# A fused two-layer block on one core: score blocks of one key tile and two heads, and an add cut in four

## The chip, the cores and the metric

The program runs on one core of a Trainium2 chip. The metric is the device time in microseconds (us) from start to end of one execution; several executions are timed and their median counts. One further execution is recorded by the hardware profiler, and the rows below come from it. The engines are called PE (TensorE, the matrix engine), DVE (VectorE), ACT (ScalarE), POOL (GpSimd) and SP (SyncE, which only issues transfers). Each works through its own queue in order, and they wait for one another by semaphores.

## The reference, cut to what matters

The input is 8 sequences ("batches") of 512 tokens with 256 features. Four blocks are added to it one after the other: an attention with hyperbolic distances, a mixture of 64 experts, a low-rank attention, and an attention with switched value experts. The change touches only the first:

```python
q, k, v = (layernorm(x) @ w.T for w in (wq, wk, wv))      # 16 heads of 16
q_norm_sq, k_norm_sq = sum(q*q), sum(k*k)
diff_sq = q_norm_sq + k_norm_sq - 2.0 * qk
denom = max((1 - q_norm_sq) * (1 - k_norm_sq), 1e-6)
cosh_arg = max(1.0 + 2.0 * diff_sq / denom, 1.0)
attn = softmax(-arccosh(cosh_arg))
x = x + (attn @ v) @ wo.T
```

With t = cosh_arg - 1, the number exp(-arccosh(1 + t)) is 1 / (1 + t + sqrt(t (t + 2))). The kernel computes it as exp(-ln(1 + (t + sqrt(t (t + 2))))).

## The kernel before

The program has three stages. Stage one holds the first attention, the router, the shared expert and the table of expert slots, for all 8 batches; stage two runs the 64 experts; stage three the two other attentions. Only stage one is changed.

Stage one is a software pipeline over batches b = -1 to 9 and, within each, over the 8 pairs of heads (p = 0 to 7). Every engine runs the same loop, `cycle(v, b, par, p, ...)`, and the order of the work on each queue is written out by hand: what a cycle always does, and between it the tasks that the tables `TO_ACT` (products that ACT takes from PSUM) and `TO_DVE` (those that DVE takes) name for that pair. A table's last column says to which batch the task belongs ("this", "before", "after", "before2"): layer norm and projections of the next batch run beside the distances of this one and the router of the one before.

The query and key vectors of a pair lie transposed in `QT` and `KT`: 54 partition rows for the even head from row 0, and 54 for the odd head from row 64 (`SL` = 64). Each head's vector is written as three parts of `QV` = 18 rows, so that a product in the faster format keeps its precision. A matmul of a 128-key tile `KT[lo:hi, pair, mt*P:(mt+1)*P]` with all 512 queries `QT[lo:hi, pair, :]` gives t itself, 128 keys by 512 queries, in one PSUM bank.

The steps of one pair:

- **PE, `scores(v, pair, r)`**, L352: four blocks r = 0 to 3 of two matmuls each, into the two PSUM tiles `SC[0]` and `SC[1]` of two banks. Block r holds head r // 2 and key tiles 0 and 1, or 2 and 3. Before it PE waits on `scores_free`, which says that the block before last was read. Blocks 0 and 1 of the next pair are issued at the end of a cycle, blocks 2 and 3 early in the pair's own.
- **DVE, `distances`**: for each block L614 writes max(t, 0) to `TT`, and L616 (t + 2) t to `SS`. `TT` is a ring of 8 heads, `SS` one of 4. `room` waits once for a pair until the ring places are free: on `pv` (attention product done) and on `w` (POOL's add done for the pair before last). `distances_slow` is the branch for clamped denominators and isn't taken with these inputs.
- **ACT, `root(v, h)`**, L780, one cycle later: square root of `SS` for one head, 128 x 2048, after `scores_free` has counted that head's two blocks.
- **POOL, `add_root(v, h)`**, L849: `TT` = `TT` + `SS` for one head, one instruction of 128 x 2048; it then increments `w`. Around it POOL has the scatter of slot numbers (L853, indirect DMAs) and two small powers for the layer norms (L843).
- **ACT, `logarithm`** (L784) and **`numerator`** (L788), another cycle later, in `TT`.
- **PE, `attend`**, L373: four steps a pair, one key tile of both heads each, summed in `OB`. `query_norms` (L359) makes one matmul for either head, at rows 0 to 53 and at rows 64 to 117.

Other work of stage one that the text names: the transposes of queries and keys (`refill`, L340) from `ST`, which DVE's `split` fills (L568 a cast, L570 and L571 differences, four instructions for a pair); transposes (L301) into `WKA`, which ACT copies to `XT` (L792); the shared expert's products (`shared`, L433 and L434, taken by DVE at L751); the projection of queries and keys (`project`, L307); `norms` (L509 to L520); `clamp_apply` (L537 to L555); `stats` and `norm` (L478 to L488, with POOL's L843 between them); and the slot numbers (`slots`, L700 to L730).

Of the kernel before, what the change touches and what calls it, by code (L numbers as in the profile page):

```python
# [19 lines left out]
ALU = mybir.AluOpType  # L20
# [3 lines left out]
P = 128  # L24
B, N, D = 8, 512, 256
T = B * N
NT = N // P
# [4 lines left out]
GH = 4  # L32
NG = H0 // GH
QV = DH0 + 2
SL = 64
RING = 2 * GH
CLAMP = 1e-6
# [33 lines left out]
class View:  # L71
# [77 lines left out]
    p=H0, pv=H0, o_sb=NG, ao=1, x1=1, var2=1, rstd2=1, xn2=1, mask=1, shifted=1, exps=1,  # L149
# [5 lines left out]
def stage_one(nc, sems, sb, ps, dram, cst, TIDF):  # L155
# [10 lines left out]
    SQ = sb("SQ", [P, 2, N])  # L166
    ST = sb("ST", [P, 2, 2, 2 * NT, SL])
    QT = sb("QT", [P, PAIRS, N], F32R)
    KT = sb("KT", [P, PAIRS, N], F32R)
    V = [sb(f"VAL{i}", [P, NT, H0, DH0 + 1]) for i in range(2)]  # L170
    TT = sb("TT", [P, RING, NT, N])
    SS = sb("SS", [P, GH, NT, N])
# [18 lines left out]
    AM = [sb(f"AM{i}", [P, 2, PAIRS, NT, 2]) for i in range(2)]  # L191
# [12 lines left out]
    SC = [ps(f"SC{i}", [P, 2, N]) for i in range(2)]  # L204
# [18 lines left out]
    def a_slot(v, parts, par, p, slot, **of):  # L223
        for at, s, name, i, whose in TO_ACT:
            if at == p and s == slot and of[whose]:
                parts[name](v, i, par)
# [6 lines left out]
    def bank_d(v):  # L233

        v.items += 1
        return WKD[v.items % 2]

    block = nc.Block()
    with block as block:
# [43 lines left out]
        def _(pe):  # L283
# [57 lines left out]
                                       ST[:, pair % 2, side, 2 * j:2 * j + 2, :].rearrange("p a b -> p (a b)"), ident[:])  # L341
                ins.then_inc(sems["refill_in"], 1)

            def scores(v, pair, r):

                h2, half = r // 2, r % 2
                lo, hi = SL * h2, SL * h2 + 3 * QV
                if v.due("scores_free", 2):
                    pe.wait_ge(sems["scores_free"], v.value)
                for m in range(2):  # L350
                    mt = 2 * half + m
                    ins = pe.matmul(SC[half][:, m, :], KT[lo:hi, pair, mt * P:(mt + 1) * P], QT[lo:hi, pair, :],  # L352
                                    start=True, stop=True)
                ins.then_inc(sems["scores"], 1)

# [116 lines left out]
        def _(dve):  # L472
# [97 lines left out]
                dve.tensor_tensor(q_st[:, :, 2 * QV:3 * QV], q, q_st[:, :, 0:QV], ALU.subtract)  # L570
                dve.tensor_tensor(k_st[:, :, QV:2 * QV], k, k_st[:, :, 0:QV], ALU.subtract).then_inc(sems["split"], 1)  # L571

            def room(v, h2):

                if h2 == 0 and v.due("pv", RING, 2):
                    dve.wait_ge(sems["pv"], v.value)
                if h2 == 0 and v.due("w", GH, 2):
                    dve.wait_ge(sems["w"], v.value)

            def distances_slow(v, par, pair):  # L580

                dve.wait_ge(sems["work_d"], v.next("work_d", 2))
                for h2 in range(2):
                    dve.tensor_scalar(SQ[:, h2, :], bank_d(v)[:], -1.0, 1.0, ALU.mult, ALU.add).then_inc(sems["took_d"], 1)
                dve.drain()
                for h2 in range(2):
                    h = 2 * pair + h2
                    tt, ss = TT[:, h % RING], SS[:, h % GH]
                    room(v, h2)
                    for half in range(2):  # L590
                        dve.wait_ge(sems["scores"], v.next("scores"))
                        for m in range(2):
                            mt = 2 * half + m
                            dve.tensor_scalar(ss[:, mt, :], SQ[:, h2, :], AM[par][:, 1, pair, mt, h2:h2 + 1], CLAMP,
                                              ALU.mult, ALU.max)
                            dve.drain()
                            dve.reciprocal(ss[:, mt, :], ss[:, mt, :])
                            dve.drain()
                            dve.scalar_tensor_tensor(tt[:, mt, :], SC[half][:, m, :], 0.0, ss[:, mt, :], ALU.max, ALU.mult)
                            dve.drain()  # L600
                            ins = dve.scalar_tensor_tensor(ss[:, mt, :], tt[:, mt, :], 2.0, tt[:, mt, :], ALU.add, ALU.mult)
                            dve.drain()
                        ins.then_inc(sems["scores_free"], 1)

            def distances(v, par, pair):

                for h2 in range(2):
                    h = 2 * pair + h2
                    tt, ss = TT[:, h % RING], SS[:, h % GH]
                    room(v, h2)  # L610
                    for half in range(2):
                        part = slice(2 * half, 2 * half + 2)
                        dve.wait_ge(sems["scores"], v.next("scores"))
                        dve.tensor_scalar(tt[:, part, :], SC[half][:], 0.0, None, ALU.max)  # L614
                        dve.drain()
                        dve.scalar_tensor_tensor(ss[:, part, :], SC[half][:], 2.0, tt[:, part, :], ALU.add, ALU.mult)\  # L616
                            .then_inc(sems["scores_free"], 1)
                    if h2 == 0:
                        dve.wait_ge(sems["work_d"], v.next("work_d", 2))
                        dve.sem_inc(sems["took_d"], 2)  # L620

# [154 lines left out]
        @block.scalar  # L776
        def _(act):
            def root(v, h):
                act.wait_ge(sems["scores_free"], v.next("scores_free", 2))
                act.activation(SS[:, h % GH], SS[:, h % GH], ACT.Sqrt).then_inc(sems["root"], 1)  # L780

            def logarithm(v, h):
                act.wait_ge(sems["w"], v.next("w"))
                act.activation(TT[:, h % RING], TT[:, h % RING], ACT.Ln, bias=1.0)  # L784

            def numerator(v, h):
                act.drain()
                act.activation(TT[:, h % RING], TT[:, h % RING], ACT.Exp, scale=-1.0).then_inc(sems["p"], 1)  # L788

            def to_xt(v, c, par):  # L790
                act.wait_ge(sems["work_a"], v.next("work_a"))
                act.activation(XT[:, c, :], WKA[:], ACT.Copy).then_inc(sems["took_a"], 1)  # L792

            def project(v, j, par):
                act.wait_ge(sems["work_a"], v.next("work_a"))
                act.activation(QK[:, :, :, j, :, 0:DH0].rearrange("p s q h d -> p (s q) h d"),
                               WKA[:].rearrange("p (g h d) -> p g h d", h=2, d=DH0), ACT.Copy).then_inc(sems["took_a"], 1)

            def refill(v, i, par):
                act.wait_ge(sems["refill_in"], v.next("refill_in"))  # L800
                act.activation((QT, KT)[i % 2][:, i // 2, :], WKA[:], ACT.Copy).then_inc(sems["took_a"], 1)  # L801

            parts = dict(turn=to_xt, turn_ao=to_xt, turn2=to_xt, turn_hid=to_xt, project=project, refill=refill)

            def cycle(v, b, par, p, **of):
                roots = of["this"] if p else of["before"]
                numerators = of["this"] if p > 1 else of["before"]
                h_root, h_num = 2 * ((p - 1) % PAIRS), 2 * ((p - 2) % PAIRS)
                a_slot(v, parts, par, p, 0, **of)
                if roots:  # L810
                    root(v, h_root)
                a_slot(v, parts, par, p, 1, **of)
                if roots:
                    root(v, h_root + 1)
                a_slot(v, parts, par, p, 2, **of)
                if p == 7 and of["before"]:
                    act.wait_ge(sems["gu"], v.next("gu"))
                    act.activation(GU[:, :, 0:F], GU[:, :, 0:F], ACT.Silu).then_inc(sems["silu"], 1)
                if numerators:
                    act.preload_act_table_set("natural_log_exp_and_others")  # L820
                    logarithm(v, h_num)
                a_slot(v, parts, par, p, 3, **of)
                if numerators:
                    numerator(v, h_num)
                a_slot(v, parts, par, p, 4, **of)
                if numerators:
                    logarithm(v, h_num + 1)
                a_slot(v, parts, par, p, 5, **of)
                if numerators:
                    numerator(v, h_num + 1)  # L830
                if p == 6 and of["before"]:
                    act.wait_ge(sems["shifted"], v.next("shifted"))
                    act.activation(LS[:], LS[:], ACT.Exp).then_inc(sems["exps"], 1)
                a_slot(v, parts, par, p, 6, **of)

            pipeline(cycle)
# [3 lines left out]
        def _(pool):  # L840
# [3 lines left out]

            def add_root(v, h):
                pool.wait_ge(sems["root"], v.next("root"))
                tt = TT[:, h % RING].rearrange("p a b -> p (a b)")
                ss = SS[:, h % GH].rearrange("p a b -> p (a b)")
                pool.tensor_tensor(tt, tt, ss, ALU.add).then_inc(sems["w"], 1)  # L849

            def scatter(v, c0):
                for c in range(c0, c0 + SCATTERS):
# [1008 lines left out]
```

## Time and profile before

| | |
|---|---|
| median of 3 runs | 3386.88 us (3384.12 to 3393.02) |
| the profiled execution's own time | 3382.55 us |
| its span, first to last instruction | 3380.4 us |
| mean granted TensorE clock | 0.814 of full speed |
| PE busy | 2684.0 us, 79% |
| PE weight loads | 1231.3 us, 36% |
| DVE busy | 2039.4 us, 60% |
| ACT busy | 1709.0 us, 51% |
| POOL busy | 1845.2 us, 55% |

Busy shares are means over the span. Stage one ends at about 1500 us. A row of a view by line and form has the line, the engine, the operation, its output and inputs with their shapes, and the count; then busy us and the mean ns of one; then the engine's idle time just before these instructions and what ended it. A row of a timeline has start, duration, engine, line, operation and count, and in brackets the idle time before it with its releaser; neighbours of one kind are drawn together.

### The profile page before, as it was taken

Reading aid. Unit: us, or ns where it says so; the run is one execution under the profiler, and the core shown is the slowest. Engines: PE = TensorE matmul, PEld = TensorE weight load, DVE = VectorE, ACT = ScalarE, POOL = GpSimd, SP = SyncE. Lnnn points to the kernel's source line nnn. Section 1 sums busy time; section 2 is a strip of 40 time slices with the busy share of each in tenths; the row PEclk is TensorE's granted clock in tenths of the full one; section 3 lists DMA queues with packets and bytes.
Section 4 is the critical chain, followed back from the end, with each engine's and each line's share of the span. In section 5 each row is a group of like instructions: output and inputs, shape, how many; then the busy total and the mean of one; then the engine's idle time right before and its main releaser. Section 6 shows DMA issues by size and latency. Waiting matters only on the chain. (4 is left out here: it accounts for less than half of the span.)

```text
span 3380.4 us, 31098 instructions
## 1 busy us (share of the span) xinstructions
PE 2684.0 (79%) x10185; PEld 1231.3 (36%) x10185; DVE 2039.4 (60%) x3044; ACT 1709.0 (51%) x2409; POOL 1845.2 (55%) x1527
## 2 busy tenths in 40 slices
PE   4677787777777677774598499989999999999984
PEld 2222333232332333222255144444444444444432
DVE  4787868687887868662133166564646565655541
ACT  1677667666666767791122154444444444444440
POOL 0444456565655555674577103583847465655585
PEclk7667676676767777666699699999999999999996
DMA  2000000000000000002599400000000000000000
GB/s 88 13 0 1 15 13 13 15 13 15 8 8 13 15 13 7 15 9 27 150 277 240 93 1 1 1 1 19 1 19 1 19 1 13 7 7 1 7 1 13
DMA packets 94880, 99.02 MB, mean 29 GB/s; under 512 B 19552, under 2 KB 91488, under 8 KB 94688
## 3 DMA queue, kind: packets, MB, share of 16 engines
q1 hardware_dynamic: 69984, 73.53, 7.5%
q0 software_dynamic: 24704, 23.22, 3.8%
q8 instruction: 84, 1.38, 0.2%
q14 instruction: 108, 0.88, 0.2%
HBM read 74.24 MB, written 26.80 MB: 30 GB/s over the span
## 5 line engine op out<-in xcount | busy, mean ns | idle before, releaser
L849 POOL TENSOR_TENSOR TT<-TT,SS 128x2048 f32<-128x2048 f32 x128 | 579.6, 4543 | 530.9 <-ACT SS L780 529.8
L1467 ACT ACTIVATE PR<-S,NM 128x512 f32<-128x512 f32 x512 | 347.6, 684 | 591.3 <-DVE NM L1588 591.3
L1588 DVE TENSOR_REDUCE NM<-S 128x2 f32<-128x1024 f32 x256 | 313.1, 1223 | 254.9 <-PE S L1382 254.7
L373 PE MATMUL OB<-TT,VAL 128*17 128x512 f32 x1024 | 386.9, 865 | 75.9 <-ACT TT L788 75.5
L614 DVE TENSOR_SCALAR TT<-SC 128x1024 f32<-128x1024 f32 x256 | 311.8, 1218 | 134.6 <-PE SC L352 75.8
L853 POOL DMA_INDIRECT slot_tokens<-TID,IDX x256 | 261.3, 1021 | 131.0 <-issue 86.8
L1382 PE MATMUL S<-KT,QT 64*128 64x512 f32 x1024 | 328.7, 662 | 0.0
L616 DVE SCALAR_TENSOR_TENSOR SS<-SC,TT 128x1024 f32<-128x1024 f32 x256 | 313.6, 1225 | 20.2 <-issue 1.3
L352 PE MATMUL SC<-QT,KT 54*128 54x512 f32 x512 | 232.6, 554 | 78.2 <-DVE SS L616 77.7
L1411 PE MATMUL OT<-PT,VN 128*64 128x512 f32 x1024 | 283.1, 632 | 3.0 <-ACT PT L1473 2.1
L1393 PEld LDWEIGHTS TP<-ident,PR 128*128 128x128 f32 x2048 | 227.3, 141 | 143.7 <-issue 118.2
L1393 PE MATMUL TP<-ident,PR 128*128 128x128 f32 x2048 | 275.4, 277 | 4.3 <-DVE PT L1593 2.6
L788 ACT ACTIVATE TT<-TT 128x2048 f32<-128x2048 f32 x128 | 244.8, 1912 | 9.2
L784 ACT ACTIVATE TT<-TT 128x2048 f32<-128x2048 f32 x128 | 243.9, 1905 | 0.7
L780 ACT ACTIVATE SS<-SS 128x2048 f32<-128x2048 f32 x128 | 242.0, 1906 | 3.7 <-DVE SS L616 2.9
L1593 DVE COPY PT<-TP 128x512 f32<-128x512 f32 x256 | 175.4, 685 | 102.3 <-PE TP L1393 99.8
L352 PEld LDWEIGHTS SC<-QT,KT 54*128 54x128 f32 x512 | 102.7, 242 | 307.7 <-DVE SS L616 211.1
L1686 POOL TENSOR_TENSOR GT<-AH,MO 128x320 f32<-128x320 f32 x224 | 156.5, 730 | 94.5 <-DVE AH L1618 86.7
L1671 POOL TENSOR_TENSOR VN<-VN,VM 128x256 f32<-128x256 f32 x256 | 186.0, 727 | 37.3 <-issue 1.3
L1651 POOL TENSOR_TENSOR rstd1b<-var1b,mhalf 128x4 f32<-128x4 f32 x16 | 16.5, 1032 | 340.9 <-DVE var1b L1533 340.9
L1473 ACT ACTIVATE PT<-TP 128x512 f32<-128x512 f32 x256 | 153.1, 598 | 57.0 <-PE TP L1393 56.2
L340 PE MATMUL WKA<-ident,ST 128*128 128x128 f32 x512 | 115.5, 366 | 83.4 <-ACT QT L801 53.0
(227 smaller groups left out, 4485.8 us busy)
## 6 DMA issues: line engine op xcount, KB each, us to landing
WG<-w_gu SPq DMA_DIRECT2D x64, 384.0 KB
WD<-w_dn SPq DMA_DIRECT2D x64, 128.0 KB
stream<-rows SPq DMA_DIRECT2D x1, 4224.0 KB, 17.2
XL<-x SPq DMA_DIRECT2D x8, 512.0 KB, 4.2
X<-x SPq DMA_DIRECT2D x8, 512.0 KB, 3.9
rows<-XL SPq DMA_DIRECT2D x8, 512.0 KB
slot_tokens<-TID,IDX POOLq DMA_INDIRECT x256
stream<-X SPq DMA_DIRECT2D x8, 512.0 KB
```

Of the source, the lines that this page charges most:

```text
L352: ins = pe.matmul(SC[half][:, m, :], KT[lo:hi, pair, mt * P:(mt + 1) * P], QT[lo:hi, pair, :], start=True, stop=True)
L373: ins = pe.matmul(OB[r:r + DH0 + 1, :], values_of[:, mt, h, :], TT[:, h % RING, mt, :], start=(mt == 0), stop=(mt == NT - 1))
L614: dve.tensor_scalar(tt[:, part, :], SC[half][:], 0.0, None, ALU.max)
L616: dve.scalar_tensor_tensor(ss[:, part, :], SC[half][:], 2.0, tt[:, part, :], ALU.add, ALU.mult)\
L788: act.activation(TT[:, h % RING], TT[:, h % RING], ACT.Exp, scale=-1.0).then_inc(sems["p"], 1)
L849: pool.tensor_tensor(tt, tt, ss, ALU.add).then_inc(sems["w"], 1)
L853: pool.indirect_dma_start(table, bass.IndirectOffsetOnAxis(ap=IDX[:, c:c + 1], axis=0), TID[:, c // K:c // K + 1], None).then_inc(sems["sc ...
L1382: ins = pe.matmul(S[s % 2][:, h2, :], QT[r % 2][lo:lo + DH1, pair, j * P:(j + 1) * P], KT[r % 2][lo:lo + DH1, pair, :], start=True, stop=True)
L1393: ins = pe.transpose(TP[h2][:, m * P:(m + 1) * P], PR[s % 2][h2][:, m * P:(m + 1) * P], ident[:])
L1411: ins = pe.matmul(OT[lo:lo + DH1, :], VN[r % 2][:, m, h * DH1:(h + 1) * DH1], PT[pair % 2][h2][:, m, :], start=(m == 0), stop=(m == NT - 1))
L1467: act.activation(PR[s % 2][h2][:], S[s % 2][:, h2, :], ACT.Exp, bias=NM[:, s % 2, h2:h2 + 1], accum_out=SM[:, pair % 2, j, h2:h2 + 1]).the ...
L1588: dve.tensor_reduce(NM[:, s % 2, :], S[s % 2][:], AX, ALU.max, negate=True).then_inc(sems["peak"], 1)
```

## The change

A score block holds one key tile of both heads instead of two key tiles of one head. Its two matmuls therefore use different row halves (0 to 53, 64 to 117). DVE's two instructions for a block still have 128 x 1024 elements, now written to two places 2048 elements apart. ACT's `root` waits once for a pair, for all four blocks, before its even head. POOL's add for one head is issued as four instructions of 128 x 512, of which the last increments `w`. The counts of all semaphores stay as they were.

```diff
-            def scores(v, pair, r):
-
-                h2, half = r // 2, r % 2
-                lo, hi = SL * h2, SL * h2 + 3 * QV
+            def scores(v, pair, mt):
+
                 if v.due("scores_free", 2):
                     pe.wait_ge(sems["scores_free"], v.value)
-                for m in range(2):
-                    mt = 2 * half + m
-                    ins = pe.matmul(SC[half][:, m, :], KT[lo:hi, pair, mt * P:(mt + 1) * P], QT[lo:hi, pair, :],
+                for h2 in range(2):
+                    lo, hi = SL * h2, SL * h2 + 3 * QV
+                    ins = pe.matmul(SC[mt % 2][:, h2, :], KT[lo:hi, pair, mt * P:(mt + 1) * P], QT[lo:hi, pair, :],
                                     start=True, stop=True)
                 ins.then_inc(sems["scores"], 1)
...
+            def tiles(pair):
+                h = 2 * pair
+                return TT[:, h % RING:h % RING + 2], SS[:, h % GH:h % GH + 2]
...
             def distances(v, par, pair):
 
-                for h2 in range(2):
-                    h = 2 * pair + h2
-                    tt, ss = TT[:, h % RING], SS[:, h % GH]
-                    room(v, h2)
-                    for half in range(2):
-                        part = slice(2 * half, 2 * half + 2)
-                        dve.wait_ge(sems["scores"], v.next("scores"))
-                        dve.tensor_scalar(tt[:, part, :], SC[half][:], 0.0, None, ALU.max)
-                        dve.drain()
-                        dve.scalar_tensor_tensor(ss[:, part, :], SC[half][:], 2.0, tt[:, part, :], ALU.add, ALU.mult)\
-                            .then_inc(sems["scores_free"], 1)
-                    if h2 == 0:
+                tt, ss = tiles(pair)
+                room(v)
+                for mt in range(NT):
+                    dve.wait_ge(sems["scores"], v.next("scores"))
+                    dve.tensor_scalar(tt[:, :, mt, :], SC[mt % 2][:], 0.0, None, ALU.max)
+                    dve.drain()
+                    dve.scalar_tensor_tensor(ss[:, :, mt, :], SC[mt % 2][:], 2.0, tt[:, :, mt, :], ALU.add, ALU.mult)\
+                        .then_inc(sems["scores_free"], 1)
+                    if mt == 1:
                         dve.wait_ge(sems["work_d"], v.next("work_d", 2))
                         dve.sem_inc(sems["took_d"], 2)
...
             def root(v, h):
-                act.wait_ge(sems["scores_free"], v.next("scores_free", 2))
+                if h % 2 == 0:
+                    act.wait_ge(sems["scores_free"], v.next("scores_free", NT))
                 act.activation(SS[:, h % GH], SS[:, h % GH], ACT.Sqrt).then_inc(sems["root"], 1)
...
             def add_root(v, h):
                 pool.wait_ge(sems["root"], v.next("root"))
-                tt = TT[:, h % RING].rearrange("p a b -> p (a b)")
-                ss = SS[:, h % GH].rearrange("p a b -> p (a b)")
-                pool.tensor_tensor(tt, tt, ss, ALU.add).then_inc(sems["w"], 1)
+                tt, ss = TT[:, h % RING], SS[:, h % GH]
+                for mt in range(NT):
+                    ins = pool.tensor_tensor(tt[:, mt, :], tt[:, mt, :], ss[:, mt, :], ALU.add)
+                ins.then_inc(sems["w"], 1)
```

## Rows read from the trace of the kernel before

**Rows 1.** The page: granted TensorE clock in 40 slices of the span.

```profile
PEclk7667676676767777666699699999999999999996
```

**Rows 2.** Windows: busy us and count of PE, PEld, DVE, ACT, POOL; clock; DMA.

```profile
800.00:990.00 190.00, 146.72 (x441) 60.81 (x441) 147.80 (x220) 129.51 (x96) 108.69 (x51) 0.69 0.07 13
...
1000.00:1022.00 22.00, 21.82 (x50) 7.79 (x50) 9.33 (x9) 8.30 (x9) 6.31 (x3) 0.50 0.07 24
1022.00:1044.00 22.00, 18.32 (x56) 7.05 (x55) 11.18 (x14) 18.58 (x14) 11.64 (x7) 0.97 0.09 25
...
1500.00:3380.00 1880.00, 1579.37 (x6903) 779.22 (x6899) 912.42 (x1388) 709.32 (x1673) 1056.28 (x1172) 0.91 0.16 40
```

**Rows 3.** Waits from 100 to 1500 us: total, times, longest.

```profile
PEld SC L352 <- DVE SS L616: 200.0, 106, 9.5
...
DVE TT L614 <- PE SC L352: 75.8, 39, 8.8
```

**Rows 4.** Lines L359, then L352: durations (min/median/max) and first and last start.

```profile
L359 PE MATMUL WKD<-QT,selq x2: 790/791/792, 999.8 to 999.8; 54*128 54x512 f32 x2
...
L352 PE MATMUL SC<-QT,KT x2: 625/708/792, 1003.6 to 1004.2; 54*128 54x512 f32 x2
```

**Rows 5.** Timeline of PE, 1027 to 1036 us.

```profile
1027.41 1.96 PE L307 MATMUL WKA<-wqkv,XT 128*128 128x512 f32 x4 [1.92 <-ACT QK L796]
...
1035.35 0.73 PE L352 MATMUL SC<-QT,KT 54*128 54x512 f32 x2
```

**Rows 6.** Groups, 100 to 1500 us (L1690: whole span); last row durations as in rows 4.

```profile
L849 POOL TENSOR_TENSOR TT<-TT,SS 128x2048 f32<-128x2048 f32 x126 | 570.6, 4543 | 530.8 <-ACT SS L780 529.8 <-issue 0.6
...
L614 DVE TENSOR_SCALAR TT<-SC 128x1024 f32<-128x1024 f32 x249 | 303.3, 1218 | 134.3 <-PE SC L352 75.8 <-POOL TT L849 50.0 <-issue 8.1
...
L568 DVE CAST ST<-QK 128x288 fp32r<-128x288 f32 x112 | 92.9, 871 | 14.1 <-PE WKA L340 13.9
...
L509 DVE TENSOR_TENSOR SQ<-QK 128x1024 f32<-128x1024 f32 x14 | 31.5, 2248 | 0.5
...
L707 DVE TENSOR_TENSOR LG<-LG,eoff 128x256 f32<-128x256 f32 x7 | 28.0, 3993 | 0.5
...
L548 DVE TENSOR_SCALAR RR<-RR 128x64 f32<-128x64 f32 x7 | 24.9, 3563 | 0.5
...
L514 DVE TENSOR_SCALAR AM<-NR 128x128 f32<-128x128 f32 x7 | 10.2, 1454 | 0.5
...
L1690 POOL TENSOR_TENSOR GO<-GO,GT 128x1280 f32<-128x1280 f32 x56 | 162.1, 2894 | 8.3 <-issue 0.4
...
L568 DVE CAST ST<-QK x128: 292/305/4673, 54.5 to 1354.2; 128x288 fp32r<-128x288 f32 x128
```

**Rows 7.** Timeline of DVE, instructions that stretch and waits at L614.

```profile
182.76 0.97 DVE L568 CAST ST<-QK 128x288 fp32r<-128x288 f32 x1
...
182.76 5.52 DVE L568 CAST ST<-QK 128x288 fp32r<-128x288 f32 x2
...
612.32 3.06 DVE L483 TENSOR_SCALAR var<-mv 128x4 f32<-128x4 f32 x1
...
1036.12 1.23 DVE L614 TENSOR_SCALAR TT<-SC 128x1024 f32<-128x1024 f32 x1 [5.93 <-PE SC L352]
...
1089.58 4.83 DVE L568 CAST ST<-QK 128x288 fp32r<-128x288 f32 x2
...
1149.03 1.23 DVE L614 TENSOR_SCALAR TT<-SC 128x1024 f32<-128x1024 f32 x1 [0.91 <-PE SC L352]
...
1157.04 4.59 DVE L707 TENSOR_TENSOR LG<-LG,eoff 128x256 f32<-128x256 f32 x1
```

**Rows 8.** Timeline of POOL, the adds beside these.

```profile
178.99 9.13 POOL L849 TENSOR_TENSOR TT<-TT,SS 128x2048 f32<-128x2048 f32 x2 [22.86 <-ACT SS L780]
...
610.80 4.55 POOL L849 TENSOR_TENSOR TT<-TT,SS 128x2048 f32<-128x2048 f32 x1 [3.91 <-ACT SS L780]
...
1084.99 9.03 POOL L849 TENSOR_TENSOR TT<-TT,SS 128x2048 f32<-128x2048 f32 x2
```

More of the change, by code:

```diff
@@ L571, in split, with room @@
                 dve.tensor_tensor(k_st[:, :, QV:2 * QV], k, k_st[:, :, 0:QV], ALU.subtract).then_inc(sems["split"], 1)
-            def room(v, h2):
-                if h2 == 0 and v.due("pv", RING, 2):
+            def tiles(pair):
+                h = 2 * pair
+                return TT[:, h % RING:h % RING + 2], SS[:, h % GH:h % GH + 2]
+            def room(v):
+                if v.due("pv", RING, 2):
                     dve.wait_ge(sems["pv"], v.value)
-                if h2 == 0 and v.due("w", GH, 2):
+                if v.due("w", GH, 2):
                     dve.wait_ge(sems["w"], v.value)
@@ L585, in distances_slow @@
                 dve.drain()
-                for h2 in range(2):
-                    h = 2 * pair + h2
-                    tt, ss = TT[:, h % RING], SS[:, h % GH]
-                    room(v, h2)
-                    for half in range(2):
-                        dve.wait_ge(sems["scores"], v.next("scores"))
[L592 to L595, printed above, removed]
-                            dve.drain()
[L597 to L603, printed above, removed]
@@ L605, in distances @@
-            def distances(v, par, pair):
[L607 to L611, printed above, removed]
-                        part = slice(2 * half, 2 * half + 2)
-                        dve.wait_ge(sems["scores"], v.next("scores"))
-                        dve.tensor_scalar(tt[:, part, :], SC[half][:], 0.0, None, ALU.max)
-                        dve.drain()
-                        dve.scalar_tensor_tensor(ss[:, part, :], SC[half][:], 2.0, tt[:, part, :], ALU.add, ALU.mult)\
-                            .then_inc(sems["scores_free"], 1)
-                    if h2 == 0:
+                tt, ss = tiles(pair)
@@ new lines, in distances_slow @@
+                room(v)
+                for mt in range(NT):
+                    dve.wait_ge(sems["scores"], v.next("scores"))
+                    for h2 in range(2):
+                        dve.tensor_scalar(ss[:, h2, mt, :], SQ[:, h2, :], AM[par][:, 1, pair, mt, h2:h2 + 1], CLAMP,
+                                          ALU.mult, ALU.max)
+                        dve.drain()
+                        dve.reciprocal(ss[:, h2, mt, :], ss[:, h2, mt, :])
+                        dve.drain()
+                        dve.scalar_tensor_tensor(tt[:, h2, mt, :], SC[mt % 2][:, h2, :], 0.0, ss[:, h2, mt, :],
+                                                 ALU.max, ALU.mult)
+                        dve.drain()
+                        ins = dve.scalar_tensor_tensor(ss[:, h2, mt, :], tt[:, h2, mt, :], 2.0, tt[:, h2, mt, :],
+                                                       ALU.add, ALU.mult)
+                        dve.drain()
+                    ins.then_inc(sems["scores_free"], 1)
@@ new lines, in distances @@
+            def distances(v, par, pair):
+                tt, ss = tiles(pair)
+                room(v)
+                for mt in range(NT):
+                    dve.wait_ge(sems["scores"], v.next("scores"))
+                    dve.tensor_scalar(tt[:, :, mt, :], SC[mt % 2][:], 0.0, None, ALU.max)
+                    dve.drain()
+                    dve.scalar_tensor_tensor(ss[:, :, mt, :], SC[mt % 2][:], 2.0, tt[:, :, mt, :], ALU.add, ALU.mult)\
+                        .then_inc(sems["scores_free"], 1)
+                    if mt == 1:
@@ L846, in add_root @@
                 pool.wait_ge(sems["root"], v.next("root"))
-                tt = TT[:, h % RING].rearrange("p a b -> p (a b)")
-                ss = SS[:, h % GH].rearrange("p a b -> p (a b)")
-                pool.tensor_tensor(tt, tt, ss, ALU.add).then_inc(sems["w"], 1)
+                tt, ss = TT[:, h % RING], SS[:, h % GH]
+                for mt in range(NT):
+                    ins = pool.tensor_tensor(tt[:, mt, :], tt[:, mt, :], ss[:, mt, :], ALU.add)
+                ins.then_inc(sems["w"], 1)
             def scatter(v, c0):
```

## The prediction

> **What bounds the kernel now.** I read the page first, for where stage one ends and what clock it has: the granted clock is 0.6 to 0.7 in the first 18 slices and mostly 0.9 after [rows 1]. The change touches nothing behind 1500 us, which is 1880 us of the span [rows 2]; all that follows is about the 1500 us before. Then windows of one batch: in 190 us PE is busy 146.7, DVE 147.8, ACT 129.5 and POOL 108.7 [rows 2]. No engine is full. The reader should see two engines at 77% that hand work to each other in queues of fixed order. Then the waits: PE's weight loads for the scores wait 200.0 us for DVE to free a block, and DVE only 75.8 us for scores [rows 3]; POOL waits 529.8 us for ACT's root [rows 6]. So DVE leads PE at most scores, and a faster score block matters where the row of DVE's wait says that PE is late. The timelines show two such places in a batch, and long stretches in which DVE goes from task to task without a wait: those are paid in DVE time.
>
> The third thing to see is in DVE's own durations. A cast of 128x288 takes 305 ns in its median, but 871 ns in the mean of 112; L707 needs 3993 ns for 256 elements a row, L548 3563 ns for 64 [rows 6]. These long ones all lie beside an add of POOL. Undisturbed, L568 has its median; L509, with as many elements as L614, has 1.22 us; L707, L548 and L514, with fewer elements than the cast, have at most its 0.3. Against these the excess of the groups is 59 (92.9 less 112 x 0.305), 14, 26, 23 and 8 us: 130 us, some 16 a batch [rows 6]. L614 and L616, which read PSUM, never stretch: 1218 ns in the mean [rows 6].
>
> **The score blocks.** The trace has both arrangements. In a score block at the lower clock (0.50 of full, the 1.2 GHz level [rows 2]) the matmuls start at 1003.6 and 1004.2, one after the other, and the second lasts 0.63 us [rows 4]: the block takes 1.22 us. The two matmuls of `query_norms`, same shape but in different row halves, start together and end after 0.79 us [rows 4]. So a block falls from 1.22 to 0.79 us at the lower clock; at the full one from 0.73 [rows 5] to about 0.50, half of what the lower level gives up (0.43), since it streams twice as fast. A mean clock of 0.69 [rows 2] is 62% of the time at 0.5; four blocks in 64 pairs are then some 90 us less PE work. Hardly any is on the path:
> - Around 1000 to 1022 us PE is busy 21.82 of 22 us [rows 2]; two blocks of pair 1 lie in that run, and it ends in transposes that ACT waits for; behind ACT's copies come the projection and then DVE's wait, 5.93 us at 1036.12 [rows 7]. Both blocks count: -0.86. The block that ends that wait, at full clock: -0.23.
> - DVE's 0.91 us wait before pair 7 [rows 7] ends with a block at full clock: -0.25.
> - In all other pairs PE waits for DVE to free the block, which costs the gain; worth 0. Were every block on the path it would be 32 x 0.35 = 11 us a batch.
>
> **DVE's two instructions** keep their 1024 elements: 0; the inner runs stay 512 long. ACT's root waits for four blocks instead of two, but comes a cycle later, behind DVE's tasks: 0. If that cover were gone, it would be one block pair, 4.9 us, for each pair; nothing shows it near.
>
> **The add in four.** L849 takes 4543 ns for 2048 elements, L1690 2894 ns for 1280 [rows 6]: 2.15 ns an element and 0.15 us besides. A piece of 512 is then 1.25 us, four are 4.98: +0.44 us a head. Lower bound +0 (4.54 / 4), upper +0.6. POOL idles 530 us before its adds [rows 6], so this is mostly hidden; behind the adds wait L843, the scatters, and DVE's `room`.
>
> What do the cuts do to the stretched DVE instructions? Here the order of turns decides. At 178.99 two adds follow each other; the boundary is near 183.5. DVE's cast comes at 182.76 and needs 0.97 us: it gets in at the boundary. The second cast, ready at once, is then held for the whole second add: both take 5.52 us [rows 7, 8]. So DVE's and POOL's instructions take turns, and each DVE instruction of this kind waits for one POOL instruction as long as POOL has one queued. With pieces, a lone DVE instruction waits 0.6 us in the mean instead of some 3. But a chain of them loses a piece at each member, and POOL's pieces wait in turn. For a chain with as many members as pieces are left, nothing is won, and DVE ends later by what POOL's adds have grown. Place by place, per batch:
> - L483 (612.32, 3.06 us) stands alone [rows 7]; behind it POOL's power for the norm, after the add of 610.80 [rows 8]. That add starts 0.86 us earlier, since two score blocks lie before ACT's root; it grows 0.44 and is held up 0.2. DVE then is bound by the power's result, not by L483: -1.7.
> - L509: two of them with a free instruction between; mean excess 1.0 us over 14 [rows 6], 1.8 a batch. One lands near the end of an add, the second in new pieces: -1.0.
> - L548, then L550, L553 and L555 as further members, four pieces left: 0.
> - L568 at 1089.58, held 4.3 us by the second add of 1084.99 [rows 7, 8]: 4.3 pieces left, eight members (two splits). Blocked time 4.3 + 0.9 of growth, and four members in it; before, these came after it. +1.0. The same at pair 6: +1.0. At pair 5 PE is later anyhow: 0.
> - L707 at 1157.04 and its neighbours, six members and more: +1.0 for the growth [rows 7].
>
> Sum for a batch: -0.86 - 0.23 - 0.25 - 1.7 - 1.0 + 2.0 + 1.0 = -1.1 us, in 8 batches -8.5. Besides, L514 was hit twice in the run for 4.3 us each (10.2 us in seven, against 0.23 each) [rows 6] and stands nearly alone: -5. Together about -13 us. The profiled execution took 3382.55 us for its span of 3380.4; the median shown is 3386.88. Against its own time the forecast is 3370, against the median 3374 us.
>
> Two rules of the Trainium skill bear on this. "SBUF — State Buffer", section "SBUF: two separate sides", says that DVE and GpSimd share a port pair as an exclusive lock held for the whole instruction; read simply, an add a quarter as long blocks a quarter as long, which is what the first rival below would be. "TensorE: Matmul & The Clock Gate", Part 1, says that the slow clock is the resting state and activity lifts it; this speaks against making PE's work denser and its pauses longer, the second rival. The trace agrees only in part: the window at 0.50 has PE busy for 99% of it, the one at 0.97 for 83% [rows 2]. By the first rule alone the time would be 3300 us, by the second alone 3417, against my 3374.
>
> **Rivals.**
> A, *the cuts free DVE*: after its turn DVE keeps the port for its next instructions, or POOL's gap between pieces lets several through. Then each of some 50 hits loses 0.6 us instead of the measured: 130 - 30 = 100 us less DVE time, of which I put three quarters on the path (DVE is busy 78% of a batch [rows 2]), and with PE's terms 3386.9 - 75 - 11 = about 3300. For it: the size of the excess. Against it: the second cast at 182.76. Chance 0.10.
> B, *the clock* (the other side): with less PE work the full-clock stretch of the projections, 1022 to 1044 at 0.97 [rows 2], stays at the lower level. Four products of 1.96 us there become 3.7 each, +7.0 us, of which PE's wait for ACT hides 1.9 [rows 5]: +5.1 us a batch, +41 in all, and with PE's terms 3386.9 + 41 - 11 = 3417. It decides as soon as a batch loses more than 1.5 us of this kind. For it: the low clock in this stage. Against it: what lifts the clock isn't the busy share. Chance 0.13.
> C, *nothing*: PE waits for DVE anyway, gains and growths cancel: 3386.9 less or more 8. Chance 0.30; the same terms as mine, with the add's growth at its upper bound or L483 and L509 gaining half.
> D, *the pieces cost more*: the pool's pieces and DVE's chains meet more often (adds are 10% longer), and the wait at `room` for pair 7, now without any, appears: +1.0 more at each of three chains and 1 us at `room`, +4 - 1 a batch: +24, 3411. Chance 0.07.
> My forecast (a gain of 10 to 35 us, its upper part if more of the 90 us of PE work proves to be on the path) has 0.40.
>
> **How the numbers follow.** A measurement of this kernel tells about 0.3%, 10 us, from no change. A and 0.36 of the forecast's 0.40 are faster: 0.46. C less a little and the forecast's edge are the same: 0.33. B, D and that little are slower: 0.21. The range goes from 3332 (half the PE work on the path, or half of A) to 3407 (half of B): outside it are A's full size and B's, about 2 in 10.
>
> **What would show it.** Score blocks of 0.79 and 0.50 us on PE, L352 starts in pairs; if not, the first step is wrong. L849 x512 at 1.25 us mean. L568's longest near 1.5 us instead of 4.7, but L570, L571, L709 to L715, which never stretched, now at over 1 us in part: that is the turn-taking; if they stay undisturbed, A is right. The clock in windows of a batch near 0.69; under 0.65 is B. DVE busy in stage one nearly unchanged. The prediction fails if PE's chain through ACT was longer on the path than two blocks a batch, or the clock moves.

## The result, and the profile after

The changed kernel takes 3293.97 us in the median of 4 runs (3291.70 to 3321.41), the kernel before 3385.61: a ratio of 0.974, 95% interval 0.969 to 0.980, or some 87 to 92 us less. Forecast were 3374 us and a range of 3332 to 3407. Direction right, size not: seven times as much as the 13 us of the sum.

The page of the changed kernel: the granted clock in 40 slices (against [rows 1]), and POOL's add.

```profile
PEclk7678787877777777775997899999999999999996
...
L848 POOL TENSOR_TENSOR TT<-TT,SS 128x512 f32<-128x512 f32 x512 | 652.1, 1308 | 401.8 <-ACT SS L779 401.5
```

Windows of the changed kernel, columns as in [rows 2]: one 190 us stretch, and the 6 us in which PE has the shared expert's products of one batch.

```profile
670.00:860.00 190.00, 132.79 (x463) 53.95 (x461) 154.12 (x240) 134.59 (x101) 124.80 (x106) 0.74 0.08 15
...
947.00:953.00 6.00, 6.00 (x24) 2.91 (x24) 4.97 (x6) 2.37 (x3) 3.74 (x4) 1.00 0.00 0
```

In a stretch as long as the one of [rows 2], PE is busy 14 us less and DVE 6 us more: more work of DVE fits in. The clock is 0.74, where it was 0.69. The second row has no like in the kernel before. The same products, L433 there and L431 here, by line (min/median/max):

```profile
L433 PE MATMUL WKD<-wdn,XT x48: 634/714/794, 440.8 to 1393.7; 128*128 128x256 f32 x48
```
```profile
L431 PE MATMUL WKD<-wdn,XT x48: 379/431/483, 416.9 to 1311.9; 128*128 128x256 f32 x48
```

All 48 between 100 and 1430 us (eight in each of six batches; L434 there and L432 here have the eight over the other rows) were at the lower clock before, and all 48 are at the full one now: the run of 16 products takes 5.1 us instead of 9.3 in each of these batches. PE's timeline just ahead of it, in the changed kernel:

```profile
942.53 1.90 PE L371 MATMUL OB<-TT,VAL 128*17 128x512 f32 x4 [0.19 <-ACT TT L787]
944.36 0.96 PE L340 MATMUL WKA<-ident,ST 128*128 128x128 f32 x4
...
945.68 1.04 PE L371 MATMUL OB<-TT,VAL 128*17 128x512 f32 x4
...
947.07 0.70 PE L431 MATMUL WKD<-wdn,XT 128*128 128x256 f32 x2
```

The attention step `L371` falls from 1.90 to 1.04 us within 3 us: the clock rises during L340, some 6 us into pair 1. Before, PE had the same work here at 0.50 for all 22 us to 1022 [rows 2].

The pairs of batches 1 to 6, mean us from the first L614 (L612) of a pair to that of the next, read off DVE's timeline of the kernels told of below; with the length of the run of shared products, the projections that follow it ("proj": `project` into WKA, four runs of four matmuls a batch, their lengths summed over the six batches; all at full clock would be 47), DVE's held time (all DVE instructions to 1500 us, what each lasts beyond the shortest of its kind in any of these kernels, where over 0.15 us), and the median. The medians come from several chips: gains are compared with the kernel before on the same chip, and not one median with another.

```
                    p0    p1    p2    p3    p4    p5    p6    p7  batch shared  proj  held  median
before             18.7  25.4  32.5  22.4  16.2  26.4  19.3  27.1  187.9   9.3    53   160    3386
change             16.9  20.7  29.5  21.6  16.5  25.8  19.9  25.5  176.4   5.1    53   140    3294
e1 blocks only     17.5  20.1  33.8  22.8  15.5  25.9  20.2  26.6  182.3   5.1    65   186    3354
e2 pieces only     17.7  26.5  30.9  22.2  17.3  26.8  19.5  26.4  187.4   9.3    57   143    3387
e5 pairs 0, 1      16.9  20.9  30.3  22.2  17.2  26.8  19.3  26.2  179.9   5.1    58   134    3339
e6 pairs 2 to 7    17.6  21.2  29.0  21.6  16.6  25.7  20.1  25.0  176.8   5.1    55   145    3317
e7 before, 1/4 add 16.9  18.8  32.1  20.1  15.2  25.5  19.3  25.3  173.3   5.1    57    15    3292
e9 filler          18.7  21.9  32.8  22.4  16.2  26.5  19.3  27.1  184.8   5.1    59   157    3378
e10 blocks twice   17.4  20.8  29.7  22.1  17.0  25.7  19.5  26.2  178.4   5.1    60   149    3325
```

Of 11.5 us a batch, 4.7 are in pair 1, where the shared products lie, 3.0 in pair 2, 3.4 in pairs 0 and 7.

The clock moves at a second place too. In the six batches of the changed kernel the projections behind the shared products are at full clock four times; twice their second and third run are mostly at the lower one:

```profile
961.51 3.19 PE L307 MATMUL WKA<-wqkv,XT 128*128 128x512 f32 x4 [3.65 <-ACT QK L795]
965.47 3.66 PE L307 MATMUL WKA<-wqkv,XT 128*128 128x512 f32 x4 [0.78 <-ACT QK L795]
```

A run of four takes 1.95 us at full clock ([rows 5] has one). In these two batches DVE's wait for scores in pair 2 is 7.7 us, in three others 4.7: what the projections take longer is on the path. The kernel before has them all at full clock in three of its six batches.

### The profile page after: what moved, and what is told of

The parts are those of the page before. It is cut to its first block and busy times, and to the rows that moved or that the text cites. A ratio compares the mean times of both kernels' runs of the same rounds, so it can differ in the third digit from the quotient of the medians.

```text
span 3289.6 us, 31482 instructions
## 1 busy us (share of the span) xinstructions
PE 2514.8 (76%) x10185; PEld 1158.7 (35%) x10185; DVE 2017.9 (61%) x3044; ACT 1706.0 (52%) x2409; POOL 1914.4 (58%) x1911
## 5 line engine op out<-in xcount | busy, mean ns | idle before, releaser
L848 POOL TENSOR_TENSOR TT<-TT,SS 128x512 f32<-128x512 f32 x512 | 652.1, 1308 | 401.8 <-ACT SS L779 401.5
L371 PE MATMUL OB<-TT,VAL 128*17 128x512 f32 x1024 | 349.4, 786 | 86.9 <-ACT TT L787 86.9
L612 DVE TENSOR_SCALAR TT<-SC 128x1024 f32<-128x1024 f32 x256 | 311.4, 1216 | 121.4 <-POOL TT L848 60.7
L614 DVE SCALAR_TENSOR_TENSOR SS<-SC,TT 128x1024 f32<-128x1024 f32 x256 | 313.5, 1225 | 20.2 <-issue 1.3
L350 PE MATMUL SC<-QT,KT 54*128 54x512 f32 x512 | 149.6, 594 | 96.1 <-DVE SS L614 95.9
L340 PE MATMUL WKA<-ident,ST 128*128 128x128 f32 x512 | 115.0, 365 | 114.9 <-ACT QT L800 78.2
L1690 POOL TENSOR_TENSOR GO<-GO,GT 128x1280 f32<-128x1280 f32 x56 | 161.9, 2892 | 8.2 <-issue 0.4
```

The source lines that it names most:

```text
L371: ins = pe.matmul(OB[r:r + DH0 + 1, :], values_of[:, mt, h, :], TT[:, h % RING, mt, :], start=(mt == 0), stop=(mt == NT - 1))
L612: dve.tensor_scalar(tt[:, :, mt, :], SC[mt % 2][:], 0.0, None, ALU.max)
L614: dve.scalar_tensor_tensor(ss[:, :, mt, :], SC[mt % 2][:], 2.0, tt[:, :, mt, :], ALU.add, ALU.mult)\
L848: ins = pool.tensor_tensor(tt[:, mt, :], tt[:, mt, :], ss[:, mt, :], ALU.add)
```

## The experiments

Each was timed beside the kernel before on its chip, whose median there was 3390 (e1 to e4), 3391 (e5 to e8), 3392 (e9 to e12) and 3397 us (e13 to e15); ratios are to that.

**The two halves apart.** e1 is the changed kernel with POOL's add whole, e2 the kernel before with the add in four.

```diff
 # e1                                        # e2: the other way round
-                for mt in range(NT):
-                    ins = pool.tensor_tensor(tt[:, mt, :], tt[:, mt, :], ss[:, mt, :], ALU.add)
+                pool.tensor_tensor(tt, tt, ss, ALU.add).then_inc(sems["w"], 1)
```

> The score blocks of the change, and POOL's add whole as before. Theory PE (the blocks in two row halves shorten PE's work, and the full clock comes earlier and holds longer): near the changed kernel, 3285 to 3305 us, clock in stage one about 0.75. Theory port (the add in four frees DVE): only the two or three blocks on the path, 3370 to 3380 us, clock 0.70.

> POOL's add in four pieces alone, score blocks as before. Theory PE: 3380 to 3400 us, no gain, since DVE's waits for POOL only change owner. Theory port: 3300 to 3320 us.

e1: 3354.03 us, ratio 0.990 (0.988 to 0.991). e2: 3386.66, 0.998 (0.997 to 1.000). Neither theory holds alone. The pieces are worth 4 to 6 us with the old blocks; the blocks are worth 36 alone; the two together 87 to 92, so that the pieces are worth 51 to 55 with the new blocks. The run of shared products is 5.1 us in e1 and 9.3 in e2. But e1 loses some of what this gives at once: its projections in pair 2 are in no batch all at full clock, 65 us over six batches, where the kernel before and the change have 53. One batch of e1, PE and then DVE's wait that follows; in a batch of the kernel before with all of them at full clock it is 5.93 us [rows 7]:

```profile
1002.83 3.75 PE L307 MATMUL WKA<-wqkv,XT 128*128 128x512 f32 x4 [0.78 <-ACT QK L795]
...
1010.78 1.22 DVE L612 TENSOR_SCALAR TT<-SC 128x1024 f32<-128x1024 f32 x1 [9.16 <-PE SC L350]
```

Up to 12 us of the pieces' 51 to 55 are therefore the clock in pair 2, which they bring back.

**Blocks that can't run side by side.** e3 and e4 (whole add) put a small product over all 128 rows between a block's two matmuls.

```diff
+                    if h2 == 1:
+                        pe.matmul(SC[mt % 2][:, 1, 0:2], onesf[:], onesf[:, 0:2], start=True, stop=True)
                     ins = pe.matmul(SC[mt % 2][:, h2, :], ...
```

> The changed kernel with a two-column product over all 128 rows (of a constant, into columns that are overwritten) between the two matmuls of each score block, so that they can't run side by side. Block 1.3 us or more at the lower clock, one more small product in each block. Theory PE: the gain is gone, 3385 to 3405 us. If the order of the blocks (one key tile of both heads) or the pieces made the gain, it stays: 3295 to 3320 us.

> As the one before, and the add whole: only the order of the blocks and ACT's wait for four of them are left of the change. Theory PE: 3385 to 3405 us. Theory order: 3295 to 3320 us. Against e3 it gives the worth of the pieces once more: theory PE within 8 us.

e3: 3429.46, 1.014 (1.011 to 1.018). e4: 3466.91, 1.022 (1.020 to 1.024). The order of the blocks alone gains nothing. Both are slower than a mere undoing should be, since the small product takes 0.38 to 0.58 us in each block; they say that PE's work is on the path when there is more of it. In e4 the shared products took 9.3 us in all six batches shown, in e3 9.3 in three and 5.1 in three: the clock has two outcomes here, and little decides. Between them the two give the pieces' worth once more, and the theory's 8 us for it is missed: 37 us, of which the shared products are some 8. The pieces thus pay with the new order of blocks also where no block runs side by side (held time 140 us in e4 and 110 in e3).

**Where the blocks must be.** e5 has the new blocks in pairs 0 and 1 only, e6 in 2 to 7 only, both with the add in four.

```diff
-                for h2 in range(2):
+                for i in range(2):
+                    h2, kt = (i, mt) if pair in PACKED else (mt // 2, 2 * (mt % 2) + i)
```

> The add in four in all pairs; score blocks of both heads in pairs 0 and 1 only, in pairs 2 to 7 two key tiles of one head as before. Theory clock (the gain of the packed blocks is mainly that the full clock is there when PE comes to the shared expert's products in pair 1): those products take 5.1 us, and the time is half way or further to the changed kernel, 3325 to 3350 us. Theory block time (each packed block gives its share): 2 pairs of 8, 3360 to 3370 us.

> The complement: blocks of both heads in pairs 2 to 7, the old ones in pairs 0 and 1; the add in four. Theory clock: the shared products stay at 9.3 us, 3350 to 3380 us. Theory block time: 3310 to 3325 us.

e5: 3338.97, 0.985 (0.982 to 0.988). e6: 3316.95, 0.977 (0.974 to 0.980). Half of the clock theory fell: e6 has no new block near the shared products, and they are at full clock all the same. So it isn't the denser blocks just ahead that lift the clock. In percent the two gains add up to 3.8, the change has 2.6; the 26 us of the shared products (6 x 4.2 and 0.4 in the seventh batch) and the pieces' 6 us stand in both, 0.9 together if they are wholly on the path, which closes most of the gap.

**What the add costs at most.** e7 is the kernel before, e8 the changed one, each with POOL adding only the first 512 of 2048 columns; the root of the other three tiles is left out.

> The kernel before, with POOL adding only the first of four key tiles (the root of the other three isn't added): one instruction of 1.2 us a head. It bounds what any cut of the add can give. If DVE's held instructions are paid on the path: 160 us less excess, 3260 to 3320 us. If they are mostly covered: above 3350 us.

> The changed kernel with only the first of the four pieces (the root of the other three tiles isn't added). Excess 140 us less. If the held instructions are paid on the path: 3200 to 3240 us; else 3270 to 3290 us.

e7: 3291.53, 0.970 (0.966 to 0.973). e8: 3255.11, 0.959 (0.956 to 0.963). With the old blocks, 145 us less held time give 100 us, up to 26 of them again the shared products at 5.1 us; after the change 121 us less held time (19 are left) give 44 to 51. DVE's held time is on the path, as the prediction said, but not microsecond for microsecond, by these runs half or less. Instead DVE waits longer for scores, 128 us against 76 with the old blocks and 122 against 51 with the new ones (100 to 1500 us).

**More work, less time.** e9 is the kernel before, with products that no one uses ahead of pair 1's query norms. e10 is the changed kernel with each block's matmuls issued twice.

```diff
 # e9, query_norms
+                    if pair == 1 and h2 == 0:
+                        for _ in range(3):
+                            pe.matmul(bank[:], ident[:], wqkv[:, 0, 0:N], start=True, stop=True)
 # e10, scores
-                for h2 in range(2):
+                for h2 in (0, 1, 0, 1):
```

> The kernel before with three products of constants, 128 x 512 in float32, ahead of pair 1's query norms, into a PSUM bank that is overwritten next: some 5 us more PE work a batch at the lower clock, just before the stretch in which the clock stayed low. Theory clock: the full clock comes in pair 1, the shared products take 5.1 instead of 9.3 us, and the time rises by no more than 10 us, or falls. Theory PE work: 20 to 40 us slower.

> The changed kernel, each block's two matmuls issued twice (the second pair overwrites the first with the same values): PE time of a block as before the change, 1.2 us at the lower clock, but in two row halves at once. Theory clock: shared products 5.1 us, 3300 to 3335 us. Theory PE work (what counts is that PE has less to do): 3370 us or more.

e9: 3377.68, 0.995 (0.993 to 0.997). e10: 3324.96, 0.980 (0.978 to 0.982). PE's timeline of e9, in a batch:

```profile
990.80 3.83 PE L362 MATMUL WKD<-wqkv,ident 128*128 128x512 f32 x6
...
996.54 0.73 PE L352 MATMUL SC<-QT,KT 54*128 54x512 f32 x2
...
998.83 0.70 PE L437 MATMUL WKD<-wdn,XT 128*128 128x256 f32 x2
```

The reader should see the filler's 3.83 us, and behind it every product of the old kernel at its full-clock length: the block 0.73 us, where the like block of the kernel before stood at the lower clock [rows 4], and the shared products 0.70 instead of 1.22. Pair 1 is 3.5 us shorter with 3.8 us more work in front of its own. Nothing else was changed: this shows the clock by itself. The net gain is 15 to 17 us, with the filler in front and the projections of pair 2 longer by 6 us over six batches. In e10 a block has its old PE time:

```profile
649.16 1.22 PE L350 MATMUL SC<-QT,KT 54*128 54x512 f32 x4 [0.86 <-DVE SS L614]
```

and 67 of the 92 us remain (by the ratios 69 of 87). The shorter block as such is worth 18 to 24 us, and a part of that is again the clock: e10's projections take 60 us where the changed kernel's take 53.

**How many pieces.** e11 has two, e12 eight.

> The changed kernel with the add in two instructions of 128 x 1024. Turn-taking with four pieces was worth 60 us over one. If the length of the piece that a held DVE instruction waits for is what counts: half way, 3305 to 3335 us, excess 155 to 170 us.

> The changed kernel with the add in eight instructions of 128 x 256: 0.7 us each, 5.7 for a head. If the length of the piece counts and POOL's time doesn't: 3270 to 3290 us. If the growth of the add by 0.7 us a head is paid: 3295 to 3320 us.

e11: 3318.34, 0.978 (0.976 to 0.980), held 173 us. e12: 3321.74, 0.979 (0.977 to 0.981), held 112 us. By ratio one, two, four and eight give 0.990, 0.978, 0.974 and 0.979. Four looks best, but its interval (0.969 to 0.980) overlaps those of two and eight. At eight, held time falls by 28 us and nothing is gained; POOL's adds grow from 652 to 734 us in sum, but that these are what costs isn't shown.

**Why the pieces pay only with the new blocks.** e13 is e9 with the add in four.

> The kernel before with the three filler products and the add in four. Theory clock first (the pieces pay only with the full clock in pair 1): 3335 to 3350 us. Theory collisions (they pay because the new blocks shift the adds): 3365 to 3378 us.

e13: 3371.55, 0.993 (0.991 to 0.996), against 0.995 for e9. The full clock in pair 1 isn't what makes them pay. (In pair 2 they lose some of it here: e13's projections take 64 us, e9's 59.) What else differs between e1 and the change is seen in DVE's timelines, for instance at one place of a batch (pair 3, `clamp_apply`): the kernel before, then e1, then the changed kernel.

```profile
1068.09 3.54 DVE L548 TENSOR_SCALAR RR<-RR 128x64 f32<-128x64 f32 x1
```
```profile
1041.53 4.16 DVE L541 TENSOR_SCALAR RR<-AM,SLOW 128x128 f32<-128x128 f32 x1
1045.77 0.95 DVE L543 RECIPROCAL RR<-RR 128x128 f32<-128x128 f32 x1
1046.80 0.20 DVE L546 TENSOR_SCALAR RR<-RR 128x64 f32<-128x64 f32 x1
```
```profile
1002.91 0.88 DVE L541 TENSOR_SCALAR RR<-AM,SLOW 128x128 f32<-128x128 f32 x1
1003.87 0.95 DVE L543 RECIPROCAL RR<-RR 128x128 f32<-128x128 f32 x1
1004.90 1.33 DVE L546 TENSOR_SCALAR RR<-RR 128x64 f32<-128x64 f32 x1
1006.30 1.24 DVE L548 TENSOR_TENSOR QK<-NR,RR 128x64 f32<-128x64 f32 x1
```

With the new blocks ACT's root, and POOL's add with it, comes 0.86 us earlier against DVE here, and the whole add now holds L541, which had just slipped through before; with pieces the reciprocal, which isn't held, runs meanwhile. The collision isn't an added one, though: the add that held L548 before (L546 in e1) holds L541 in its place, and from the start of this instruction to that of the last of `clamp_apply` it is 5.6 us before, 6.0 in e1, 4.8 in the changed kernel and 5.5 in e2. So the pieces save 1.2 us a batch here with the new blocks and 0.15 with the old: a part of the answer. In all, the new blocks with the whole add have 26 us more held time than the kernel before (186 against 160), most of it at the cast into `ST` (14 us) and at the slot numbers' L703 (7), and the pieces take off 46; with the old blocks they take off 17. At half a microsecond for each, as in e7 (100 less 26, over 145), the 46 us would be some 23 of the pieces' 51 to 55, an estimate; with the 12 of the clock in pair 2, a third stays open.

**Filling PE's pauses.** e14 and e15 were meant to lengthen the full clock in the changed kernel, with four products before the transpose of the extremes, and (e15) three more ahead of pair 0's query norms.

> The changed kernel with four filler products in PE's pause of 6.3 us before the transpose of the extremes (end of pair 2). If the full clock then lasts into pair 3: 3 us less a batch, 3265 to 3285 us. If the clock doesn't change there: 3290 to 3305 us.

> As e14, and three filler products ahead of pair 0's query norms, where PE waits for ACT and DVE. If the clock comes earlier in pair 0: another 2 us a batch less than e14; if not, equal to e14 or up to 20 us more.

e14: 3307.67, 0.975 (0.972 to 0.977). e15: 3312.49, 0.976 (0.974 to 0.979). No gain: by its windows the clock in e14 stays up until about the start of pair 3 and then falls as before, and pair 3 takes 21.6 us in both. Of the kernels that do the whole work none beats the change.

## Why the prediction was wrong, point by point

*Where the missing 75 us are.* In the prediction's sum the blocks were -11 us and the pieces -3 (+0.3 a batch, and -5 for L514). Measured, the blocks alone give 36 (e1) and the pieces on top of them 51 to 55. Two steps failed: that the clock stays as it was, and that the pieces can be priced at the adds' old places. The last lines of the prediction name the first one as what would sink it.

*The score blocks' own time: right.* In the changed kernel two matmuls of a block start together and the block takes 0.79 us at the lower clock, 0.50 at the full one, as said.

```profile
L350 PE MATMUL SC<-QT,KT x2: 790/791/792, 995.0 to 995.0; 54*128 54x512 f32 x2
```

*"Hardly any is on the path": mis-sized.* The terms -0.86, -0.23 and -0.25 are 11 us in all; e10 puts the shorter blocks at 18 to 24.

*The clock: the first step that failed.* The prediction had the clock in windows of a batch "near 0.69", and as its second rival a clock that stays low for want of work, at 3417 us. It rose to 0.74, and with it the run of shared products fell from 9.3 to 5.1 us in six batches and by 0.4 us in the seventh: 26 us of PE time. e9 has the same fall with no other change than products for no one. The 22 us at 0.50 with PE busy throughout were in [rows 2]; what those products would take at the other level, and what it would be worth if the level changed, was not worked out. The clock was priced in one direction only, at +41 us. In that direction the rival came about in part: in e1 projections of pair 2 do fall to the lower clock, 2 us of PE time a batch in the mean against its 5.1, and in two batches of the changed kernel too. Whether for want of work, as the rival has it, isn't shown.

*The order of turns: right in the main.* L570 and L571 (L568 and L569 now), never stretched before, each wait about a piece, and so do the members of the chain in `slots`. The changed kernel in pair 6, and below it the casts of e2, with the old blocks:

```profile
1071.93 1.59 DVE L566 CAST ST<-QK 128x288 fp32r<-128x288 f32 x2
1073.60 1.22 DVE L568 TENSOR_TENSOR ST<-QK,ST 128x144 f32<-128x144 f32 x1
1074.74 1.37 DVE L569 TENSOR_TENSOR ST<-QK,ST 128x144 f32<-128x144 f32 x1
```
```profile
L568 DVE CAST ST<-QK x112: 296/304/9222, 170.0 to 1354.0; 128x288 fp32r<-128x288 f32 x112
```

The turns aren't strict. The prediction had the longest cast "near 1.5 us"; nearly all are at most that, but one of e2's lasts 9.22 us, from 1085.07 us on, held over eight pieces of POOL one behind another, and one of the changed kernel's 5.82 us, over five. Why DVE gets no turn there isn't shown.

Total held time fell by only 20 us (160 to 140), so the first rival's picture, in which the cuts set DVE free, is wrong though its 3300 us was near the time. That is luck: its way to the number isn't what happened. With the old blocks the pieces' sum of about zero was nearly met: 4 to 6 us (e2). The prediction's 130 us of excess is less than the 160 because it left out L483 and L705.

*Its price with the new blocks: the second step that failed.* The terms were set against the adds where they stood in the trace of before. The prediction moved one of them by 0.86 us, ahead of L483, and let it gain there, but not the one beside L543, where the same 0.86 us moves the collision from L548 to L541 (e1: 23 us of held time at L541, 19 fewer at L546), nor those at the casts and the slot numbers. The pieces' worth must be read against e1, not against the kernel before: 51 to 55 us, for terms of -3 in all. What they bring is in part held time and in part the clock in pair 2; by e3 and e4 it doesn't need blocks that run side by side.

*The piece:* 4.96 us for four undisturbed ones, 4.98 predicted; 1308 ns in the mean with DVE's turns.

A rough tally, whose terms may overlap: 26 us for the shared products at full clock, if all of it is on the path; 18 to 24 for PE's shorter blocks; at most 20 for less held time. This is 64 to 70 of 87 to 92 us; the rest isn't settled. Nor is what lifts the clock in pair 1: e6, e7, e9 and e10 lift it with different edits, e2 and e4 don't.

## What to carry to other kernels

Where a long run of products stands at one clock level, price it at the other level too before forecasting anything near it, in both directions: a small shift in the work before it can change the level. Here the change won 26 us of PE time at one such run, and e1 lost 12 at the next. When two edits come together, take the second one's price from the trace as the first one leaves it. An instruction that holds up another engine, once cut, pays by what it would otherwise hold, and more cuts don't always give more: eight gave no more than four.

## What the runs showed that was not expected

- Products that no one uses made the kernel 0.5% faster (e9), by lifting the granted clock from 0.50 to 1.00 ahead of 16 products.
- The granted clock has two outcomes at one place with nearly the same work: 22 us of a busy TensorE at 0.50 before, full level after some 6 us in the changed kernel, and each in three batches of e3.
- The same edit can lift the clock at one run of products and lower it at the next: e1 has its shared products at full clock in six batches and its projections, some 10 us later, in none wholly; behind them DVE waits up to 9.2 us for scores, where it waits 5.9 in a batch of the kernel before with all of them at full clock.
- DVE and POOL mostly took turns instruction by instruction at pieces of 0.7, 1.25 and 2.4 us alike. The Trainium skill, "SBUF — State Buffer", section "SBUF: two separate sides", has the lock held for a whole instruction, which the traces bear out; who gets it next they show besides: mostly the other engine, when it waits, but in e2 a cast of DVE was held 9.22 us over eight of POOL's pieces in a row.
